# An AdaLN block on one core: the attention state two steps ahead, n1 + 1 for the column sums, new engine orders

## Chip, core and metric

One core of a Trainium2 chip runs the whole kernel. The metric is the device time of one execution in microseconds (us). The engines are TensorE (PE in the profile, its weight loads PEld), VectorE (DVE), ScalarE (ACT), GpSimd (POOL) and SyncE (SP), which issues most DMAs.

## What is computed

All data are float32: 16 sequences of 256 tokens, width 128.

```
mod = silu(c) @ wmod -> per sequence: sa, ca, ga, sb, cb, gb;  ga, gb kept at least 0.25 from 0
h  = LN(x) * (1 + ca) + sa
Q, K = elu(h@Wq + bq) + 1, elu(h@Wk + bk) + 1;  V = h@Wv + bv;  16 heads of 8
att = Q (K^T V) / (Q . sum_tokens K + 1e-6), per head
y  = LN(h + att@Wo + bo) * g1 + beta1
z  = LN(y + relu(y@W1 + b1)@W2 + b2) * g2 + beta2
x2 = x + ga * z
h2 = LN(x2) * (1 + cb) + sb;  mixes of h2 with the token before it, for receptance and key
out = x2 + gb * sigmoid(mix_r@Wr) * (relu(mix_k@Wk')^2 @ Wv')
```

## The kernel before

A sequence is two chunks of 128 tokens. `steps(step)` on each engine runs `step(t)` for t = 0 to 16, and each engine's `step` holds an order written out by hand; semaphores, counted by sequence, tie the engines together (`need`). Step t works on several sequences at once:

- sequence t, the front: n1 = LN(x) without its affine part (`next_n1`, scale from GpSimd's `norm_scale`), turned on TensorE (`transpose_in`, L932), `hT` by ScalarE (L284), keys (L1015 bias, L1018) and queries (L1023), `exp_k`, `exp_q`, `relu_q`, `k_sb`, `qT`. Then the state: n1^T k (L1049), the sum of k over tokens (GpSimd adds the two chunks into `k_pair`, L467, and TensorE multiplies by ones, L1060), ScalarE's `a_sb` (L328), the product with `wv_mod` (L1078), `kv_raw` by VectorE (L773: adds ksum times a row of `bv_row`), and GpSimd's two multiplies by the head mask into `kvs` (L475, L481).
- sequence t - 1, attention: reading the state (L1008), `den`, `rden`, `att`, turned, `attT` (L314), the projection with the residual (L937, L1055), statistics and `ny`.
- sequence t - 2, feed-forward: ny turned, `x1T` (L288), four hidden products (L975), `hid` by ScalarE (L311, L316, L320), the way out (L943), statistics of z.
- sequence t - 3: `centred`, `middle` (x2), n3.
- sequence t - 4, mix: n3 turned, three `keepT` of ScalarE (L273, L276), `mixT` of VectorE (L672), key (L962) and receptance (L966), relu, square, tanh, value (L1087), `prod`, `take_out`, store.

Of two neighbouring statistics and their aggregate VectorE mostly does something else between. Step 8 (MIX_AT) has two GpSimd operations, `mix_now` and `mix_prev`, for the end. Rows of bv and the gates come through DRAM: TensorE's small product, a store by SP, broadcast loads (`bv_row`, `gm_rows`) in BV_PARTS and GM_PARTS. The last sequences are drained by code of their own behind `steps`: sequence 13 by mixes, 14 and 15 by products with split weights on h2, and 15 in halves (`z_norm_of_last` and others). `keep_warm` multiplies a tile of ones to nothing.

## Time and profile before

| | us |
|---|---|
| median of 3 runs | 173.39 |
| lowest, highest | 173.34, 176.28 |
| the profiled execution | 173.09 |
| its span, first to last instruction | 171.4 |
| TensorE, VectorE, ScalarE, GpSimd busy | 160.8, 137.3, 107.3, 106.8 |

The span is counted from the first to the last instruction; some 1.7 us of the execution lie around it. A busy time sums an engine's instructions without their overlaps; a wait is given with what released it.

### The profile page before, as it was taken

To read this page: it belongs to the slowest core of one execution; us is meant where nothing else is said; L and a number is where in the kernel's file an instruction comes from. 1 tells how busy PE (TensorE), PEld (TensorE's weight loads), DVE (VectorE), ACT (ScalarE), POOL (GpSimd) and SP (SyncE) were. 2 spreads that over 40 slices of the span, in tenths; PEclk is the share of its full clock that TensorE was granted. 3 is DMA by queue.
4 is the path that set the end of the run, shared out by engine and by line. 5 is a ranking of instruction groups with operands and counts; after the bars stand their busy time and mean duration, and the time that the engine had idled before them with its cause. 6 is when DMAs were issued, how large, how long until landed. Compare 5 with 4: busy or idle time off the path is not lost. (4 is left out here: it accounts for less than half of the span.)

```text
span 171.4 us, 4095 instructions
## 1 busy us (share of the span) xinstructions
PE 160.8 (94%) x1181; PEld 148.7 (87%) x1181; DVE 137.3 (80%) x618; ACT 107.3 (63%) x294; POOL 106.8 (62%) x235
## 2 busy tenths in 40 slices
PE   7995899999999999999989999999999999998883
PEld 7784689889999999999979999999999999787672
DVE  3644885989797979889896979797989788777852
ACT  3152573839393949586774949493939495737552
POOL 5233435575677777767695868676777756683531
PEclk9999999999999999999999999999999999999999
DMA  4529929900010101000010101010101010010012
GB/s 134 193 57 345 306 69 299 399 11 4 2 34 0 31 0 33 4 12 22 0 33 0 33 4 33 0 34 0 33 0 34 0 32 4 2 31 25 6 34 61
DMA packets 8347, 10.08 MB, mean 59 GB/s; under 512 B 723, under 2 KB 6534, under 8 KB 8326
## 3 DMA queue, kind: packets, MB, share of 16 engines
q1 hardware_dynamic: 7856, 9.54, 17.6%
q10 hardware_dynamic: 438, 0.28, 0.6%
q8 instruction: 10, 0.16, 0.4%
q14 instruction: 11, 0.09, 0.2%
q0 software_dynamic: 32, 0.01, 0.0%
HBM read 7.69 MB, written 2.13 MB: 57 GB/s over the span
## 5 line engine op out<-in xcount | busy, mean ns | idle before, releaser
L943 PE MATMUL bank<-w,hid 128*128 128x128 f32 x240 | 31.4, 275 | 0.0
L284 ACT ACTIVATE hT<-bank,modT 128x256 f32<-128x256 f32 x16 | 9.0, 565 | 35.4 <-PE bank L932 35.4
L975 PE MATMUL bank<-x1T,w 128*128 128x256 f32 x120 | 30.9, 380 | 0.0
L943 PEld LDWEIGHTS bank<-w,hid 128*128 128x128 f32 x240 | 29.0, 192 | 0.0
L975 PEld LDWEIGHTS bank<-x1T,w 128*128 128x128 f32 x120 | 21.5, 190 | 2.5 <-ACT x1T L288 0.2
L432 POOL TENSOR_TENSOR rstd_n<-vare_n,power 128x2 f32<-128x2 f32 x30 | 21.3, 708 | 2.4
L430 POOL TENSOR_TENSOR vare_n<-mv_n,eps 128x2 f32<-128x2 f32 x30 | 6.0, 200 | 18.9 <-DVE mv_n L540 18.9
L546 DVE TENSOR_SCALAR ny<-bank,mv_ny,rstd_ny 128x128 f32<-128x128 f32 x32 | 11.7, 406 | 5.4 <-POOL rstd_ny L432 5.4
L276 ACT ACTIVATE keepT<-bank,modT 128x255 f32<-128x255 f32 x28 | 14.3, 563 | 0.6 <-PE bank L932 0.6
L531 DVE BATCH_NORM_STATS2 stats_z<-bank 128x6 f32<-128x128 f32 x30 | 7.4, 289 | 8.2 <-PE bank L943 8.1
L430 POOL TENSOR_TENSOR vare_z<-mv_z,eps 128x2 f32<-128x2 f32 x14 | 2.8, 197 | 17.9 <-DVE mv_z L540 17.9
L932 PE MATMUL bank<-ident,n 128*128 128x128 f32 x62 | 12.0, 275 | 1.0 <-DVE n L546 0.8
L320 ACT ACTIVATE hid<-bank,b_cols 128x256 f32<-128x256 f32 x30 | 12.7, 484 | 0.0
L450 POOL TENSOR_TENSOR out_sb<-x,prod 128x256 f32<-128x256 f32 x15 | 10.9, 728 | 2.1 <-DVE prod L667 2.0
L672 DVE SCALAR_TENSOR_TENSOR mixT<-bank,modT,keepT 128x256 f32<-128x256 f32 x28 | 12.1, 472 | 0.0
L1008 PE MATMUL bank<-kvs,qT 128*128 128x144 f32 x64 | 10.6, 288 | 1.5 <-issue 1.5
L432 POOL TENSOR_TENSOR rstd_ny<-vare_ny,power 128x2 f32<-128x2 f32 x16 | 11.1, 694 | 1.2
L1055 PE MATMUL bank<-kqvo,attT 128*128 128x128 f32 x64 | 11.5, 275 | 0.0
L647 DVE SCALAR_TENSOR_TENSOR x<-z,rstd_z,xb 128x128 f32<-128x128 f32 x30 | 10.8, 401 | 0.9 <-POOL out_sb L450 0.7
L300 ACT ACTIVATE exp_k<-bank,neg 128x256 f32<-128x256 f32 x16 | 7.7, 481 | 5.5 <-PE bank L1018 5.5
L443 POOL TENSOR_TENSOR xb<-x_all,gm_rows 128x256 f32<-128x256 f32 x15 | 10.9, 727 | 0.0
L1049 PEld LDWEIGHTS bank<-k_sb,n 128*128 128x128 f32 x64 | 9.5, 191 | 1.4 <-DVE k_sb L733 0.6
(176 smaller groups left out, 480.1 us busy)
## 6 DMA issues: line engine op xcount, KB each, us to landing
gm_rows<-mod_rows_dram SPq DMA_DIRECT2D x2, 960.0 KB, 9.0
out<-out_sb SPq DMA_DIRECT2D x15, 128.0 KB, 1.8
gm_rows<-mod_rows_dram SPq DMA_DIRECT2D x1, 768.0 KB, 6.2
w<-in_w SPq DMA_DIRECT2D x1, 512.0 KB, 4.9
bv_row<-bv_rows_dram SPq DMA_DIRECT2D x1, 512.0 KB, 11.7
x_all<-in_x SPq DMA_DIRECT2D x1, 384.0 KB, 4.4
bv_row<-bv_rows_dram SPq DMA_DIRECT2D x1, 384.0 KB, 5.5
gm_rows<-mod_rows_dram SPq DMA_DIRECT2D x1, 384.0 KB, 4.7
```

What stands on the lines that cost most here:

```text
L276: nc.scalar.activation(keepT[:, i, 1:L], banks[2][:, 0:L - 1], ACT.Identity, scale=mod_col(KEEP + i, s), bias=mod_col(SB, s)).then_inc((ke ...
L320: last = nc.scalar.activation(hid[:, f, :], hidden_bank(t)[:, (f - 2) * L:(f - 1) * L], ACT.Relu, bias=b1_cols[:, f:f + 1])
L432: nc.gpsimd.tensor_tensor(rstd[name][:, :], vare[name][:, :], power[:, :], ALU.pow).then_inc(rstd_ok[name], 1)
L443: nc.gpsimd.tensor_tensor(tile[:, :, :], x_all[:, NC * s:NC * (s + 1), :], gm_rows[:, s, GB_ROW:GB_ROW + 1, :].broadcast_to([128, NC, D]), ...
L450: nc.gpsimd.tensor_tensor(out_sb[s % 2][:, :, :], x2[s % 2][:, :, :], prod[:, :, :], ALU.add).then_inc(out_ok, 1)
L546: last = nc.vector.tensor_scalar(dest[:, c, :], source(c), mv[name][:, c, 0:1], rstd[name][:, c:c + 1], ALU.subtract, ALU.mult)
L647: last = nc.vector.scalar_tensor_tensor(x2[s % 2][:, c, :], z1[:, c, :], rstd["z"][:, c:c + 1], xb[:, c, :], ALU.mult, ALU.add)
L672: nc.vector.scalar_tensor_tensor(mixT[:, i, :], banks[2][:, 0:L], modT[:, MOVE + i, s:s + 1], keepT[:, i, :], ALU.mult, ALU.add).then_inc( ...
L932: last = nc.tensor.transpose(bank[:, c * 128:(c + 1) * 128], tile[:, c, :], ident[:, :])
L943: last = nc.tensor.matmul(banks[6][:, c * D:(c + 1) * D], hid[:, f, c * 128:(c + 1) * 128], w2[:, f, :], start=False, stop=(f == FF - 1 an ...
L975: return nc.tensor.matmul(bank[:, f % 2 * L:(f % 2 + 1) * L], w1[:, f * 128:(f + 1) * 128], x1T[:, :], start=True, stop=True)
L1055: last = nc.tensor.matmul(banks[1][:, c * D:(c + 1) * D], attT[:, c * 128:(c + 1) * 128], wo, start=False, stop=(c == NC - 1))
```

## The change

- **n1 + 1.** `first_scale` on GpSimd forms std and mean - std besides rstd, so that `take_n1` writes n1 + 1. Each token's row of n1 + 1 sums to 128, so the state product with a `wv_plus` of 144 columns (the last 16 are 1/128) yields ksum too. `k_pair`, the product with ones, `kv_raw` and both mask multiplies go; `plus_row` (GpSimd) adds bv's row to `wv_mod`, and `take_kvs` (VectorE) masks all 144 columns at once. The shift and bv's row are corrected by the same 1.
- **Two steps ahead.** The step works on t (front), t - 2 (attention), t - 3 (feed-forward), t - 4 (x2, n3), t - 5 (mix); `hT`, `qT`, `kvs`, `x2` have three buffers.
- **Orders.** All engines have new orders; step(t) runs for t = 4 to 17, and the first four steps are written out. Statistics and aggregate are one call (`y_norm`, `z_norm`, `n3_norm`, `first_stats`).
- **Start.** For sequences 0 and 1 wv_plus is formed directly (`direct_rows`, `direct_weights`); the products for the biases go ahead of the modulation; SP's loads have another order, and mix_w goes from ScalarE's queue to SP's. Several `keep_warm` go.
- **End.** Sequence 13 uses the split weights too; the order of the last pieces is new.

```diff
-BV_PARTS = ((0, 2), (2, 8), (8, 16))
+BV_PARTS = ((2, 4), (4, 9), (9, 16))
...
@@ sync
+            sp.dma_start(x_all[:, NC:2 * NC, :], x_dram[:, NC:2 * NC, :]).then_inc(x_in[1], 16)
             sp.dma_start(kqvo[:, 2:4, :], a["kqvo"][:, 2:4, :]).then_inc(wvo_loaded, 16)
-            sp.dma_start(x_all[:, NC:4 * NC, :], x_dram[:, NC:4 * NC, :]).then_inc(x_in[1], 16)
+            sp.dma_start(x_all[:, 2 * NC:4 * NC, :], x_dram[:, 2 * NC:4 * NC, :]).then_inc(x_in[2], 16)
             sp.dma_start(wmod[:, 2 * D:], a["wmod"][:, 2 * D:]).then_inc(wmod_loaded[1], 16)
+            sp.dma_start(w12[:, :, :], a["w12"]).then_inc(w12_loaded, 16)
+            sp.wait_ge(bv_ok, 1)
+            sp.dma_start(scratch["bv"], bv_rows[:, :]).then_inc(bv_stored, 16)
+            sp.dma_start(mix_w[:, :, :], a["mix_w"]).then_inc(mix_loaded, 16)
+            sp.wait_ge(bv_stored, 16)
+            load_bv(0)
+            sp.dma_start(x_all[:, 4 * NC:, :], x_dram[:, 4 * NC:, :]).then_inc(x_in[3], 16)
+            sp.wait_ge(rows_ok, 1)
+            sp.dma_start(scratch["rows"], mod_rows[:, :, :]).then_inc(rows_stored, 16)
+            load_bv(1)
+            sp.wait_ge(rows_stored, 16)
+            load_gm(0)
+            load_bv(2)
...
@@ scalar: head, then step
+            take_hT(0); exponent_k(0); take_hT(1)
+            act.wait_ge(bq_ok, 1)
+            exponent_q(0); take_a(0); positive_q(0); exponent_k(1)
...
+            take_x1T(0)
+            hidden(0, 0); hidden(0, 1); take_attT(1); hidden(0, 2); hidden(0, 3)
+            modulate_wv(4); modulate_wv(5)
+            step: take_x1T(sd) take_hT(sa) hidden(sd, 0) keeps(sc) take_attT(sb_) exponent_k(sa)
+                  hidden(sd, 1..3) positive_kk(sc) take_a(sa) square_kk(sc) exponent_q(sa)
+                  positive_q(sa) tanh_of_r(sc) modulate_wv(sa + 2)
...
@@ gpsimd
+            def first_scale(s):
+                nc.gpsimd.tensor_tensor(vare["n1"][:, :], mv["n1"][:, :, 1], eps[:, :], ALU.add).then_inc(vare_ok["n1"], 1)
+                nc.gpsimd.tensor_tensor(rstd["n1"][:, :], vare["n1"][:, :], power[:, :], ALU.pow).then_inc(rstd_ok["n1"], 1)
+                nc.gpsimd.tensor_tensor(std_n1[:, :], vare["n1"][:, :], rstd["n1"][:, :], ALU.mult).then_inc(std_ok, 1)
+                nc.gpsimd.tensor_tensor(mean_n1[:, :], mv["n1"][:, :, 0], std_n1[:, :], ALU.subtract).then_inc(mean_ok, 1)
+            def plus_row(s):
+                nc.gpsimd.tensor_tensor(wv_plus[s % 2][:, 0:D], wv_mod[s % 2][:, :], bv_row[:, s, :], ALU.add).then_inc(wvp_ok, 1)
-                    nc.gpsimd.tensor_tensor(k_pair[:, :], k_sb[:, 0, :], k_sb[:, 1, :], ALU.add).then_inc(pair_ok, 1)
+            step: norm_scale("z", sp_) take_out(sc - 1) gate_weights(sc) norm_scale("n3", sp_)
+                  plus_row(sa + 1) norm_scale("ny", sb_) x_plus_shift(sd) first_scale(sa + 2)
...
@@ vector: head in part, then step
+            def take_kvs(s):
+                need(dve, u_mm, s - 2)
+                need(dve, kv_mm, s + 1)
+                nc.vector.tensor_tensor(kvs[s % 3][:, :], banks[3][:, 0:D + H], mask[:, :], ALU.mult).then_inc(kvs_ok, 1)
+            take_n1(1); take_k(0); first_stats(2); take_q(0); direct_weights(1); take_kvs(0)
+            take_n1(2); take_k(1); denominators(0); attention(0); first_stats(3); take_q(1)
...
+            y_norm(1); shift_columns(); z_norm(0); take_ny(1)
+            step: centred(sp_) denominators(sb_) attention(sb_) middle(sp_) n3_norm(sp_) mixes(sc)
+                  take_k(sa) take_n3(sp_) y_norm(sb_) take_n1(sa + 1) first_stats(sa + 2)
+                  take_ny(sb_) take_kvs(sa) take_q(sa) z_norm(sd) gated(sc)
...
+            vare_of("z", whole, LAST); centred(s14); middle(s14); n3_norm(s14)
+            vare_of("n3", whole, LAST); z_norm_of_last(0); centred_last(0)
+            nc.vector.scalar_tensor_tensor(shift_n3[:, :], mv["n3"][:, :, 0], -1.0, rstd["n3"][:, :], ALU.mult,
+                                           ALU.mult).then_inc(shift_ok, 1)
+            z_norm_of_last(1); middle_last(0)
...
@@ tensor
+            def state(s):
+                need(pe, a_ok, s + 1)
+                nc.tensor.matmul(banks[3][:, 0:D + H], a_sb[:, :], wv_plus[s % 2][:, :], start=True, stop=True).then_inc(kv_mm, 1)
-                    nc.tensor.matmul(banks[3][:, D:D + 1], k_pair[:, :], ones[:, :], start=True, stop=True).then_inc(aks_mm, 1)
+            turn_n1(0); direct_rows(); bv_product(); key_of(0); query_of(0); turn_n1(1)
+            key_by_n1(0); key_of(1); state(0); query_of(1); turn_n1(2); read_state(0)
+            key_by_n1(1); second_modulation(); state(1); key_of(2); query_of(2); turn_att(0)
+            key_by_n1(2); projection(0); state(2); turn_n1(3); hidden_bias(); key_of(3)
+            query_of(3); turn_gates(); key_by_n1(3); state(3); turn_ny(0); read_state(1)
+            hidden_products(0); turn_att(1); feed_forward_out(0, 0, 2); projection(1)
+            feed_forward_out(0, 2, FF); turn_ny(1)
+            step: turn_n1(sa) read_state(sb_) hidden_products(sd) turn_att(sb_) key_of(sa)
+                  query_of(sa) projection(sb_) mix_key(sc) mix_receptance(sc) key_by_n1(sa)
+                  feed_forward_out(sd, 0, 2) state(sa) feed_forward_out(sd, 2, FF)
+                  value_product(sc) turn_ny(sb_) turn_n3(sp_)
...
+            key_of_h2(s13); turn_n3(s14); receptance_of_h2(s13); key_of_h2(s14)
+            value_product(s13); transpose_last(0); receptance_of_h2(s14); transpose_last(1)
+            key_last(0); value_product(s14); key_last(1); receptance_last(0)
+            value_last(0); receptance_last(1); value_last(1)
```

In the diff each call stands on a line of its own; several are written on one line here, and a step's order is given by its calls, with sa = t, sb_ = t - 2, sd = t - 3, sp_ = t - 4, sc = t - 5.

## Rows read from the trace of the kernel before

**Rows 1.** The page: busy time of each engine, and the granted clock in 40 slices

```profile
PE 160.8 (94%) x1181; PEld 148.7 (87%) x1181; DVE 137.3 (80%) x618; ACT 107.3 (63%) x294; POOL 106.8 (62%) x235
...
PEclk9999999999999999999999999999999999999999
```

**Rows 2.** Windows by stage: us, busy us (instructions) of each engine, PEclk, DMA, GB/s

```profile
6.80:46.10 39.30, 35.93 (x264) 32.01 (x264) 30.14 (x137) 21.73 (x56) 19.82 (x45) 1.00 0.50 164
46.10:145.80 99.70, 98.86 (x760) 94.68 (x760) 86.95 (x390) 70.38 (x198) 71.26 (x157) 1.00 0.06 16
```

**Rows 3.** Timeline of TensorE, steady steps: start us, us, engine, line, op, tiles, count

```profile
46.15 0.38 PE L932 MATMUL bank<-ident,n 128*128 128x128 f32 x2
...
55.12 0.38 PE L932 MATMUL bank<-ident,n 128*128 128x128 f32 x2
...
97.31 0.28 PE L1060 MATMUL bank<-ones,k_pair 128*128 128x1 f32 x2
97.45 0.68 PE L962 MATMUL bank<-mixT,mix_w 128*128 128x256 f32 x2
97.96 0.61 PE L966 MATMUL bank<-mix_w,mixT 128*128 128x128 f32 x4
...
98.62 0.39 PE L1078 MATMUL bank<-wv_mod,a_sb 128*128 128x128 f32 x2
98.85 1.06 PE L943 MATMUL bank<-w,hid 128*128 128x128 f32 x8
...
103.22 1.46 PE L975 MATMUL bank<-x1T,w 128*128 128x256 f32 x6
104.51 0.38 PE L932 MATMUL bank<-ident,att 128*128 128x128 f32 x2
```

**Rows 4.** Timeline of all engines, a steady step and the drain

```profile
73.27 0.49 DVE L531 BATCH_NORM_STATS2 stats_z<-bank 128x6 f32<-128x128 f32 x2 [0.67 <-PE bank L943]
...
73.68 0.40 DVE L667 SCALAR_TENSOR_TENSOR prod<-tanh_r,bank 128x256 f32<-128x256 f32 x1
...
74.01 0.56 ACT L288 ACTIVATE x1T<-bank,beta_b,cols 128x256 f32<-128x256 f32 x1
...
75.45 0.48 ACT L300 ACTIVATE exp_k<-bank,neg 128x256 f32<-128x256 f32 x1
...
146.97 1.56 PE L975 MATMUL bank<-x1T,w 128*128 128x256 f32 x6
...
154.68 0.48 DVE L531 BATCH_NORM_STATS2 stats_z<-bank 128x6 f32<-128x128 f32 x2
...
155.27 0.25 DVE L540 BATCH_NORM_AGGREGATE mv_z<-stats_z 128x2 f32<-128x6 f32 x2
```

**Rows 5.** Groups of GpSimd instructions by line and shape, us, mean ns, idle before

```profile
L432 POOL TENSOR_TENSOR rstd_n<-vare_n,power 128x2 f32<-128x2 f32 x30 | 21.3, 708 | 2.4
...
L481 POOL TENSOR_TENSOR kvs<-kv_raw,headmask 128x128 f32<-128x128 f32 x16 | 7.3, 456 | 3.1 <-DVE kv_raw L773 2.9
...
L430 POOL TENSOR_TENSOR vare_ny<-mv_ny,eps 128x2 f32<-128x2 f32 x16 | 3.3, 204 | 2.6 <-DVE mv_ny L540 2.6
```

**Rows 6.** Timeline of TensorE, step 8: the column sum

```profile
88.23 0.38 PE L1060 MATMUL bank<-ones,k_pair 128*128 128x1 f32 x2 [0.84 <-POOL k_pair L467]
```

**Rows 7.** Timeline of all engines, start

```profile
7.35 0.56 ACT L284 ACTIVATE hT<-bank,modT 128x256 f32<-128x256 f32 x1 [4.05 <-PE bank L932]
...
10.04 0.71 PE L1049 MATMUL bank<-k_sb,n 128*128 128x128 f32 x4 [0.36 <-DVE k_sb L733]
...
13.92 0.35 DVE L773 SCALAR_TENSOR_TENSOR kv_raw<-bv_row,a_sb,bank 128x128 f32<-128x128 f32 x1 [2.54 <-DMA bv_row<-bv_rows_dram]
...
14.90 0.73 PE L1008 MATMUL bank<-kvs,qT 128*128 128x144 f32 x4 [1.46 <-issue]
```

**Rows 8.** Timeline of all engines, end

```profile
158.88 0.29 DVE L788 BATCH_NORM_STATS2 stats_z<-bank 128x6 f32<-128x128 f32 x1
...
168.99 0.29 DVE L839 TENSOR_TENSOR out_last<-x_end,prod_last 128x128 f32<-128x128 f32 x1
```

More of the change, by code:

```diff
@@ L49, in build @@
         mix_w = sb("mix_w", [128, 3, D])
-        wrT, wkT, wvT = (mix_w[:, i, :] for i in range(3))
+        wvT = mix_w[:, 2, :]
         cols = sb("cols", [128, COLS])
@@ L210, in build @@
         block = ctx.enter_context(nc.Block())
+        s13, s14 = LAST - 2, LAST - 1
+        whole, half = slice(0, NC), [slice(c, c + 1) for c in range(NC)]
         @block.sync
@@ new lines, in hidden, with keeps @@
+            def hidden(s, f):
+                if f % 2 == 0:
+                    need(act, (w1a_mm, w1b_mm)[f // 2], s + 1)
+                bank = (banks[7], banks[6])[f // 2]
+                ins = nc.scalar.activation(hid[:, f, :], bank[:, f % 2 * L:(f % 2 + 1) * L], ACT.Relu, bias=b1_cols[:, f:f + 1])
+                if f % 2 == 1:
+                    ins.then_inc((hida_ok, hidb_ok)[f // 2], 1)
+            def keeps(s):
+                need(act, mix_ok, s)
+                need(act, h2T_mm, s + 1)
+                nc.scalar.activation(keepT[:, :, 0:1], modT[:, FIRST:FIRST + 2, s:s + 1], ACT.Copy)
+                for i in range(2):
+                    last = nc.scalar.activation(keepT[:, i, 1:L], banks[2][:, 0:L - 1], ACT.Identity, scale=mod_col(KEEP + i, s),
+                                                bias=mod_col(SB, s))
+                last.then_inc(keep_ok, 1)
@@ new lines, in turn_att, with projection @@
+            def turn_att(s):
+                need(pe, att_ok, s + 1)
+                need(pe, hT_ok, s + 3)
+                need(pe, reluk_ok, s - 3)
+                transpose_in(banks[0], att, attT_mm)
+            def projection(s):
+                need(pe, attT_ok, s + 1)
+                for c in range(NC):
+                    residual_into(banks[1], hT[s % 3], c)
+                    last = nc.tensor.matmul(banks[1][:, tokens(c)], attT[:, tokens(c)], wo, start=False, stop=(c == NC - 1))
+                last.then_inc(y_mm, 1)
@@ L941, in feed_forward_out, with hidden_products @@
+            def hidden_products(s):
+                for f in range(FF):
+                    hidden_product(s, f, (banks[7], banks[6])[f // 2])
+            def feed_forward_out(s, f0, f1):
+                if f0 == 0:
+                    need(pe, hidb_ok, s + 1)
+                    for c in range(NC):
+                        residual_into(banks[6], x1T, c)
                 for f in range(f0, f1):
                     for c in range(NC):
-                        last = nc.tensor.matmul(banks[6][:, c * D:(c + 1) * D], hid[:, f, c * 128:(c + 1) * 128], w2[:, f, :],
-                                                start=False, stop=(f == FF - 1 and c == NC - 1))
```

1332 lines of the change are left out of this document (708 added, 624 removed).

## The prediction

> **What bounds the kernel now.** I began with the page [rows 1]: TensorE is busy 94% of the span, VectorE 80%, ScalarE and GpSimd some 62%; the clock stays at the upper level, 2.4 GHz. I then cut the span into stages [rows 2]. From 46.1 to 145.8 us TensorE is busy 98.86 of 99.70 us; from 6.8 to 46.1 it is busy 35.93 of 39.30 us, and part of that are products that only keep it busy. Two neighbouring rows of the turning of n1 stand 8.97 us apart [rows 3]: that is the steady period. So there only work taken off TensorE, or an engine that becomes slower than it, moves the time; at both ends it is the waits.
>
> **Steady step.** The column-sum product and its successor need 0.14 us (97.31 to 97.45) and 0.51 us (97.45 to 97.96) [rows 3]. Two passes of 256 columns alone take a third of 1.30 us, 0.43 us, as six pass in that time (the attention rows follow 1.29 us behind the hidden ones). So the sum costs 0.14 + 0.08 = 0.22 us, of which I take 0.21. The state product's two passes of 128 columns take 0.23 us (98.62 to 98.85); with 144 it is an eighth more, 0.03 us. The new period is 8.97 - 0.21 + 0.03 = 8.79 us, if nothing waits.
>
> Does anything wait? Counted from the new step's first instruction, TensorE reads the state at 0.22, starts the hidden products at 0.71, turns attention at 2.44, projects at 3.64, mixes at 4.31, multiplies key by n1 at 5.18, the state at 6.73, and turns ny at 8.31. A result must be there some 0.15 us ahead: after a wait the load is exposed (six passes take 1.56 instead of 1.46 us) and the release costs 0.05 [rows 4].
> - x1T: turning ny ends at 8.69; ScalarE's 0.56 us and the release give 9.34. Due 9.34. No slack.
> - attT: ScalarE takes hidden 0 at 1.78, then three keeps (1.44 us from x1T's start at 74.01 to exp_k's at 75.45, of which I give x1T 0.45: 0.99 us [rows 4]), then attT until 3.52; due 3.49. Loss 0 to 0.05 us.
> - k_sb: VectorE mixes from 3.27, takes k and ends at 4.5; the receptance product of the mix needs its bank at 4.7. Slack 0.15 to 0.2.
> The state itself is now two steps ahead and has whole microseconds.
>
> VectorE works 86.95 us in this stage of 11.12 steps, 7.8 us a step [rows 2]. The multiply that replaces kv_raw has about its size. But statistics and their aggregate now stand side by side in all four norms, and so do den, reciprocal and attention. An instruction that depends on nothing starts 0.41 us behind a pair of statistics (73.27 to 73.68); a dependent one 0.59 us (154.68 to 155.27) [rows 4]; with one wait in place of two I take 0.54. Four times 0.13 is 0.5 us: 8.3 of 8.79 us. It still fits, with waits of 0.5 us in all; below, a rival starts here. The bounds: 0 and 4 x 0.18 + 0.2 = 0.9 us.
>
> The Trainium skill ("VectorE: DVE Perf Modes", section on the DRAIN you can't avoid) says that the pipe empties behind every operation and that a semaphore adds nothing to it. By that rule the new order would cost VectorE nothing. The trace differs (0.41 against 0.59 us), so the measurement decides.
>
> GpSimd loses the mask multiply of kvs (456 ns), the pair sum of the same size and the small one for the sums, and gains std and mean at about the 200 ns of vare each, and wv_plus at 456 ns [rows 5]: 0.1 to 0.3 us less. In step 8 its two mix_now operations hold the column sum and TensorE for 0.84 us and a further 0.3 us of lateness [rows 6]; no sum hangs behind them now, but z's rstd does. I keep 0.5 of 1.1 us. ScalarE has the same work in another order.
>
> **Start.** TensorE now waits for wq and bq's product first, then the modulation; n1 of step 0 needs std and mean too. I put hT(0) at 8.0 against 7.35 us [rows 7]. The bv round trip, for which VectorE and TensorE wait 2.54 and 1.46 us [rows 7], is gone: direct rows serve steps 0 and 1. SP's reordered loads (x of step 1 ahead of Wv and Wo, w12 early, mix_w behind the bv store) all land ahead of their new users; if one does not, only the later x blocks, whose 1.5 MB stand behind a store, could cost 1 us. But the order by hand opens other waits. GpSimd's four dependent operations, 0.27 + 0.75 + 0.26 + 0.20, give a mean 1.5 us behind the aggregate (durations of 0.20 and 0.71 [rows 5] and a release of 0.05 each). VectorE stands at take_n1(1) until 10.6 and only then takes k(0), ready at 9.9: it gets out at 11.5 (before, TensorE used it at 10.04 [rows 7]). Carried through the queues with the durations above, TensorE waits:
> n1(1) 1.6; hT(1) 0.3; n1(2) 1.2; a(1) 0.3; k(2) 0.6; k(3) 0.5; a(3) 0.8; x1T(0) 0.4; the second half of hidden(0), which ScalarE takes behind attT(1), 1.5; ny(1), whose statistics, scale and normalising form one chain behind projection(1) and behind shift_columns and z_norm(0) in VectorE's queue, 2.4; step 4 0.6. Sum 10.2 us.
> Against that stands useful work only. By its passes (0.22 us for two of 128 columns, 0.43 for two of 256, as above) a front is 1.89, an attention 1.60, a feed-forward 3.73 and a mix 1.53 us; five fronts, three attentions and two feed-forwards are 21.7 us, the modulation, bias, gate and direct products 4.4. From 7.5 this gives 7.5 + 21.7 + 4.4 + 10.2 = 43.8 us for the start of step 5. The kernel before starts its step 5 at 46.15 [rows 3], but by then has done one attention, one feed-forward and one mix more: 6.8 us. So the start loses 6.8 - 2.35 = 4.5 us.
>
> **Sum.** Steps 5 to 15 are eleven: 43.8 + 11 x 8.79 + 0.5 = 141.0 us for the start of step 16.
>
> **End.** There remain two attentions, three feed-forwards, five mixes and doubled products for three sequences instead of two, 24.4 us of TensorE work against 17.2. Now ScalarE does keeps between hidden(0) and attT with no front to fill it: twice 1.0 us. x1T follows turn_ny at once: 0.2, 0.2 and 0.7. The last feed-forward waits for ScalarE 0.3. I reach the statistics of the last z's first half 20.1 us behind that start, at 161.1; before they stood at 158.88 [rows 8]. From there the chain to the last add took 10.4 us before [rows 8]. Now shift_n3 stands behind z_norm_of_last(0), so n3(14), its turning and h2 come after; but the key and receptance of 13 fill TensorE meanwhile, and value(14) waits for a square that ScalarE does behind both halves of h2(15). I reach 10.7. End at 141.0 + 30.8 = 171.8 us, against 169.3. The same store follows.
>
> The profiled execution took 173.09 us (span 171.4), 0.3 us under the median of 173.39, less than the runs differ among themselves; I make no correction: 173.09 + 2.5 = **175.6 us**. In parts: start +4.5, steady -11 x 0.18 - 0.6 = -2.6, end +0.6. My own bounds for the first are +2 to +6, for the last -1 to +2.5. A measurement of this kernel can tell about 2% (3.5 us) from no change: under 169.9, over 176.9.
>
> **Rivals.**
> 1. VectorE becomes the bound. If the side-by-side dependencies cost 0.9 us and the waits for u and keeps don't shift together, a step is 9.1 us: 11 x 0.31 = 3.4 more, 179.0 us. For it: 8.3 of 8.79 us full, and attT, x1T with no slack. Against: nothing forces the waits to add. It decides from a period above 8.97. Chance 0.20.
> 2. The start is as dense as before, and the whole is faster. If the chain at n1(1) and the one at ny(1) are shorter than I have them, and TensorE's holes in the start are no larger than today's, the 4.5 us fall away: 171.1 us. It decides where the start loses under 2.0 us. For it: the bv stall is gone and the state is early. Against: eleven named waits. Below 169.9 it comes only with a shorter end as well. Chance 0.24.
> 3. The cut isn't worth what the rows say: the period stays 8.97, as passes elsewhere stretch or attT's 0.05 and x1T's wait come in each step: +2.0, 177.6 us. Chance 0.08.
> 4. The holes bring TensorE's clock down. Before, the hole of 1.46 us left it at 2.4 GHz [rows 1, 7], with extra products put in between; the new start has fewer of them and holes of 1.5 and 2.4 us. At 1.2 GHz passes take twice as long, so one step's worth (8.8 us) done at half rate for 3 us costs 1.5 to 3: 178.0 us. No row shows the lower level. Chance 0.04.
> The Trainium skill ("TensorE: Matmul & The Clock Gate", section on what's actually happening) holds that an idle array falls to half rate and that activity lifts it again. The trace of before, never below full, can't show the fall.
>
> **How the numbers follow.** My forecast has 0.44, with its own range 173.5 to 177.5. The range of 8 in 10 reaches down to rival 2's 171.0 and up to 178.8. Faster by over 2%: half of rival 2's spread below and little else, 0.11. Slower: rival 1 (0.18), rivals 3 and 4 (0.07), the top of the forecast (0.03): 0.28. Within 2%: 0.61.
>
> **What would show it.** A period of turning n1 of 8.79 us with TensorE full shows the cut right; 9.0 or more with VectorE idle near zero shows rival 1. hT(1) at 11.8, exp_k(3) at 23 and step 5's turn at 43.8 test the start; idle rows of TensorE behind hid and ny rows of about 1.5 and 2.4 us test the two largest holes. In the end, attT waits of 1 us in steps 16 and 17, statistics of the last z at 161. The forecast is wrong if the start's holes sum to under 7 or over 13 us, or if a steady row waits in every step.

## The result, and the profile after

The change made the kernel slower: 183.16 us median (181.24 to 184.5, 4 runs) against 173.45 for the kernel before in the same series. The ratio is 1.048 (95% interval 1.0435 to 1.052); every ratio here is formed from the runs within 1.5% of the fastest of their kernel, which for the changed kernel are only 181.24 and 182.08. I had forecast 175.6 us, range 171.0 to 178.8. The profiled execution took 184.5 us, the longest of the four; its span is 182.8. What follows explains that execution; where the two shorter ones gained their 3 us was not recorded.

Page of the kernel after, busy time of each engine and the granted clock in 40 slices:

```profile
PE 167.7 (92%) x1147; PEld 147.5 (81%) x1147; DVE 146.1 (80%) x623; ACT 106.9 (58%) x290; POOL 103.6 (57%) x233
...
PEclk9999999969999999999999999999999999999999
```

Against [rows 1], TensorE has 34 instructions fewer and is busy 6.9 us longer, and VectorE is busy 8.8 us longer. One slice of the clock, some 37 to 41 us into the span, is no longer 9. The windows of the kernel after, to the start of step 5, from there to the start of step 16, the end, and one steady step (us, busy us and instructions of TensorE, its weight load, VectorE, ScalarE, GpSimd; clock, DMA share, GB/s):

```profile
0.00:47.10 47.10, 39.21 (x225) 32.86 (x226) 29.21 (x145) 18.74 (x48) 17.55 (x51) 0.96 0.52 164
47.10:148.70 101.60, 100.32 (x739) 90.69 (x737) 93.71 (x387) 70.89 (x196) 69.12 (x152) 1.00 0.05 14
148.70:182.80 34.10, 28.15 (x188) 23.95 (x186) 23.22 (x93) 17.29 (x47) 16.93 (x31) 1.00 0.08 24
111.97:121.04 9.07, 9.07 (x69) 8.26 (x68) 8.68 (x37) 6.45 (x18) 6.47 (x15) 1.00 0.05 14
```

All three parts came later than forecast: step 5 at 47.05 us instead of 43.8, step 16 at 148.7 instead of 141.0, and the last add ends 31.7 us behind that instead of 30.8. The three errors are 3.25, 4.45 and 0.9 us, which is 8.6 of the 8.9 us between the forecast and the profiled execution.

**The steady period.** It is the distance between rows of turning, which answer to [rows 3] (the four passes of a row here turn n3 and then n1; the rows begin steps 7 to 10, and a step proper begins 0.22 us later, with n1):

```profile
64.90 0.60 PE L1058 MATMUL bank<-ident,n 128*128 128x128 f32 x4
73.99 0.60 PE L1058 MATMUL bank<-ident,n 128*128 128x128 f32 x4
83.26 0.60 PE L1058 MATMUL bank<-ident,n 128*128 128x128 f32 x4
93.83 0.60 PE L1058 MATMUL bank<-ident,n 128*128 128x128 f32 x4
```

Over the whole stage the distance is mostly 9.01 to 9.09 us, where I had 8.79 and the kernel before 8.97; it is 9.27 and 9.37 once each, and 10.57 from step 9 to step 10, behind GpSimd's work at the end of its step 8. VectorE's timeline in one step of 9.07 us shows no wait at all in its rows:

```profile
111.78 0.49 DVE L629 BATCH_NORM_STATS2 stats_z<-bank 128x6 f32<-128x128 f32 x2
112.30 0.25 DVE L636 BATCH_NORM_AGGREGATE mv_z<-stats_z 128x2 f32<-128x6 f32 x2
...
113.50 0.35 DVE L689 RECIPROCAL rden<-den 128x32 f32<-128x32 f32 x1
113.96 0.49 DVE L695 TENSOR_TENSOR att<-bank,rden 128x128 f32<-128x128 f32 x2
114.36 0.81 DVE L728 SCALAR_TENSOR_TENSOR x<-z,rstd_z,xb 128x128 f32<-128x128 f32 x2
...
117.14 0.65 DVE L642 TENSOR_SCALAR n<-x,mv_n,rstd_n 128x128 f32<-128x128 f32 x2
117.72 0.48 DVE L629 BATCH_NORM_STATS2 stats_ny<-bank 128x6 f32<-128x128 f32 x2
118.23 0.25 DVE L636 BATCH_NORM_AGGREGATE mv_ny<-stats_ny 128x2 f32<-128x6 f32 x2
118.40 0.57 DVE L663 TENSOR_SCALAR n<-x_all,mean_n,rstd_n 128x128 f32<-128x128 f32 x2
118.89 0.48 DVE L629 BATCH_NORM_STATS2 stats_n<-x_all 128x6 f32<-128x128 f32 x2
...
119.65 0.73 DVE L642 TENSOR_SCALAR ny<-bank,mv_ny,rstd_ny 128x128 f32<-128x128 f32 x2
```

Note what the window says of the same step: TensorE busy 9.07 of 9.07 us, VectorE 8.68. Read alone, that says TensorE bounds the step. It does not: with the same products the steady step takes 8.77 us in another kernel below. A short wait ahead of a weight load does not show in the busy time, since the ends of TensorE's products are modelled.

**The start.** TensorE's timeline, the waits over 1 us that I had named, and what follows the longest:

```profile
16.96 0.44 PE L1058 MATMUL bank<-ident,n 128*128 128x128 f32 x2 [1.01 <-DVE n L663]
...
31.98 0.44 PE L1063 MATMUL bank<-ident,x1T 128*128 128x128 f32 x2 [1.26 <-ACT hid L321]
...
36.90 0.44 PE L1058 MATMUL bank<-ident,ny 128*128 128x128 f32 x2 [2.04 <-DVE ny L642]
...
38.05 3.52 PE L1142 MATMUL bank<-x1T,w 128*128 128x256 f32 x8
...
47.76 1.94 PE L1142 MATMUL bank<-x1T,w 128*128 128x256 f32 x8
```

The holes are there, near their forecast sizes of 1.2, 1.5 and 2.4 us. But the hidden products behind the third take 3.52 us, and 1.94 in the next step. The granted clock is 0.50 from 38 to 41 us. Eight passes at half rate, 1.2 GHz, are rival 4, which I had given 0.04. The very first products run at half rate too:

```profile
5.59 0.58 PE L1197 MATMUL bank<-cols,kqvo 128*128 128x1 f32 x2 [0.69 <-DMA kqvo<-in_kqvo]
...
8.93 0.66 PE L1058 MATMUL bank<-ident,n 128*128 128x128 f32 x2 [0.23 <-DVE n L844]
...
10.91 1.22 PE L1078 MATMUL bank<-kqvo,hT 128*128 128x128 f32 x4
...
14.28 0.71 PE L1078 MATMUL bank<-kqvo,hT 128*128 128x128 f32 x4
```

In the kernel before hT(0) was taken at 7.35 [rows 7], behind n1(0) turned at 6.87; here n1(0) is turned at 8.93, and four passes take 1.22 us until about 13 us, then 0.71. The clock's column reads 1.00 for this first stretch, so the half rate is read from the durations. The kernel before begins at half rate as well: two warming products take 0.77 us at 5.41 and 0.49 at 6.54, so there the rate rose at about 6 us. "Never below full", as the prediction has it, is what the column said and not what the rows say.

### The profile page after: what moved, and what is told of

It reads as the page before. It is cut to its first block, busy times and chain, and to the rows that moved or that the text cites. A ratio compares the mean times of both kernels' runs of the same rounds, so it can differ in the third digit from the quotient of the medians.

```text
span 182.8 us, 4107 instructions
## 1 busy us (share of the span) xinstructions
PE 167.7 (92%) x1147; PEld 147.5 (81%) x1147; DVE 146.1 (80%) x623; ACT 106.9 (58%) x290; POOL 103.6 (57%) x233
## 4 chain that ended last, share of the span: by engine, by line
PE 55%; DVE 26%; issue 6%; ACT 5%; POOL 4%; DMA 2%; SPq 0%; DVEq 0%; POOLq 0%; ACTq 0%
PE bank L1142 11%; PE bank L1158 9%; PE bank L1058 5%; PE bank L1180 3%; PE bank L1078 3%; PE bank L1063 3%; PE bank L1190 3%; PE bank L1114 3%; DVE stats_n L629 2%; PE bank L1173 2%; PE bank L1128 2%; PE bank L1097 2%; DVE x L728 2%; DMA kqvo<-in_kqvo 2%; DVE mixT L745 2%
## 5 line engine op out<-in xcount | busy, mean ns | idle before, releaser
L1142 PE MATMUL bank<-x1T,w 128*128 128x256 f32 x128 | 32.9, 402 | 0.7 <-ACT x1T L314 0.7
L321 ACT ACTIVATE hid<-bank,b_cols 128x256 f32<-128x256 f32 x60 | 25.2, 479 | 13.8 <-PE bank L1142 13.8
L1142 PEld LDWEIGHTS bank<-x1T,w 128*128 128x128 f32 x128 | 24.0, 198 | 4.8 <-ACT x1T L314 1.8
L314 ACT ACTIVATE x1T<-bank,beta_b,cols 128x256 f32<-128x256 f32 x16 | 9.0, 565 | 23.4 <-PE bank L1058 23.4
L504 POOL TENSOR_TENSOR vare_ny<-mv_ny,eps 128x2 f32<-128x2 f32 x16 | 3.4, 210 | 27.0 <-DVE mv_ny L636 27.0
L512 POOL TENSOR_TENSOR rstd_n<-vare_n,power 128x2 f32<-128x2 f32 x15 | 13.6, 907 | 1.2
L728 DVE SCALAR_TENSOR_TENSOR x<-z,rstd_z,xb 128x128 f32<-128x128 f32 x30 | 12.2, 446 | 1.6 <-POOL rstd_z L506 1.1
L504 POOL TENSOR_TENSOR vare_n<-mv_n,eps 128x2 f32<-128x2 f32 x14 | 2.8, 197 | 16.4 <-DVE mv_n L636 16.4
L1058 PE MATMUL bank<-ident,n 128*128 128x128 f32 x62 | 10.7, 284 | 1.5 <-DVE n L663 1.0
L1128 PE MATMUL bank<-kqvo,attT 128*128 128x128 f32 x64 | 11.5, 275 | 0.0
L1097 PE MATMUL bank<-k_sb,n 128*128 128x128 f32 x64 | 10.3, 285 | 0.8 <-DVE k_sb L670 0.8
L1114 PE MATMUL bank<-kvs,qT 128*128 128x144 f32 x64 | 10.6, 289 | 0.0
L1078 PE MATMUL bank<-kqvo,hT 128*128 128x128 f32 x64 | 10.6, 290 | 0.0
```

The costliest lines, as they stand in the source:

```text
L321: ins = nc.scalar.activation(hid[:, f, :], bank[:, f % 2 * L:(f % 2 + 1) * L], ACT.Relu, bias=b1_cols[:, f:f + 1])
L512: nc.gpsimd.tensor_tensor(rstd["n1"][:, :], vare["n1"][:, :], power[:, :], ALU.pow).then_inc(rstd_ok["n1"], 1)
L728: last = nc.vector.scalar_tensor_tensor(x2[s % 3][:, c, :], z1[:, c, :], rstd["z"][:, c:c + 1], xb[:, c, :], ALU.mult, ALU.add)
L1058: last = nc.tensor.transpose(bank[:, tokens(c)], tile[:, c, :], ident[:, :])
L1078: nc.tensor.matmul(banks[4][:, tokens(c)], hT[s % 3][:, tokens(c)], wk, start=(c == 0), stop=False)
L1097: last = nc.tensor.matmul(banks[3][:, 0:D], n1[s % 2][:, c, :], k_sb[:, c, :], start=(c == 0), stop=(c == NC - 1))
```

## The experiments

Each ratio is to the kernel before, in runs on the same chip. The changed kernel run again is the base of the first group.

**0. The changed kernel again** (no edit).

> The changed kernel again, unchanged, for a profile beside its variants. All theories: 181 to 184.5 us, steady period 9.07 us (turning of n1), a hole of about 2 us ahead of turning ny(1) and, behind it, the lower TensorE clock for about 3.5 us; the raise of the clock near the start as late as 13 us instead of 6. If the runs' difference of 3 us is the clock's alone, the lowered stretch lies elsewhere or is longer or shorter in this profile.

Measured: 183.81 us, ratio 1.057 (1.050 to 1.064). Periods mostly of 9.0 to 9.1, step 5 at 47.6. The steady step repeats; the clock does not. This time the first products were at the full rate at 5.85 us, and the granted clock was at 0.50 three times: from 8 to 11.5 us, from 18.3 to 21.7 (2.4 us behind a wait of 1.01 for n1(2)) and from 38.8 to 42.2, behind the hole at ny(1).

**1. Filling TensorE's holes in the start.**

```diff
-            keep_warm(WARM)
+            keep_warm(WARM + 4)
...
             feed_forward_out(0, 2, FF)
+            keep_warm(9)
             turn_ny(1)
```

> Four more products of ones in the wait for wq at the start, nine in the hole ahead of turning ny(1); nothing else. Theory clock: TensorE is at 2.4 GHz from about 7 us on and never falls; 1.8 us come back behind ny(1) and 2 to 2.5 at the start, together 3 to 4.5 us less than the changed kernel. Rival (the start is set by the chains through VectorE and GpSimd, the clock only fills their shadow): under 1 us less. Both: steady period unchanged, 9.07.

Measured: 182.00 us, 1.049 (1.043 to 1.055), 1.8 us less than the changed kernel, though the two intervals overlap. TensorE's timeline (the program's nine products are 18 of the profile's):

```profile
34.76 2.17 PE L1018 MATMUL bank<-warm 128*128 128x128 f32 x18
36.96 0.44 PE L1058 MATMUL bank<-ident,ny 128*128 128x128 f32 x2
...
38.11 1.99 PE L1142 MATMUL bank<-x1T,w 128*128 128x256 f32 x8
```

With products in the hole the eight passes behind it take 1.99 us instead of 3.52. The Trainium skill ("TensorE: Matmul & The Clock Gate", section on what's actually happening) says that an idle array drops to half rate; these rows agree. It does not drop every time. The hole of 2.04 us stands unfilled in nine profiles of this document; in seven the eight passes behind it take 2.89 to 3.52 us, in those of experiments 2 and 10 they take 1.99. What decides it is not shown.

The expectation held in this one place only. At the start the first products now run at the full rate from 5.64 us, but the clock fell to 0.50 from 18 to 21.6 us instead, and the wait at n1(1) grew from nothing to 1.39: n1(4) is turned at 37.23, no earlier than the 37.17 before. So the 3 to 4.5 us of the expectation were not there.

**2. VectorE's old order, statistics and aggregates apart.** An independent instruction stands between the statistics and the aggregate of n3, y, x and z again; of these the place of y's:

```diff
-                    y_norm(sb_)
+                    need(dve, y_mm, sb_ + 1)
+                    norm_stats("ny", lambda c: y[:, c, :])
+                if live(sa + 2):
...
+                    norm_stats("n1", x_chunk(sa + 2))
+                if live(sb_):
+                    norm_mv("ny", sb_ + 1)
```

> In VectorE's step alone, statistics and aggregate are taken apart again (the half of the mix, the statistics of the next x and the gated product stand between). Theory VectorE-bound by dependent neighbours: VectorE is 0.4 us freer, the receptance product of the mix no longer waits, and the period falls from 9.07 to 8.80 +- 0.05; the whole is 2.5 to 3.5 us less. Rival (VectorE is late because ScalarE's keeps come late, or because its operations stretch beside GpSimd): period 9.0 or more, under 1 us less.

Measured: 190.93 us, 1.096 (1.087 to 1.105). That is 7 us slower. VectorE now waits twice in every step:

```profile
100.04 0.65 DVE L642 TENSOR_SCALAR n<-x,mv_n,rstd_n 128x128 f32<-128x128 f32 x2 [0.47 <-POOL rstd_n L506]
...
102.80 0.73 DVE L642 TENSOR_SCALAR ny<-bank,mv_ny,rstd_ny 128x128 f32<-128x128 f32 x2 [0.53 <-POOL rstd_ny L506]
```

An aggregate taken later gives GpSimd the variance later, and VectorE stands at the scaling. So GpSimd's answer is a term of VectorE's step. The cost of the dependent neighbours is not refuted by this: from one n3 pair to the next it is 9.71 us, and without the two waits of 0.47 and 0.53 it is 8.71, or 0.36 less than 9.07. That is the 0.4 us expected; the waits took back more than twice as much. The two waits are where the theory of experiments 6 and 7 comes from.

**3. The mixing weights multiplied out in the head instead of step 8.**

```diff
-                if t == MIX_AT:
-                    nc.gpsimd.tensor_tensor(mix_now[:, :, :], mix_w[:, 0:2, :],
...
+            pool.wait_ge(mix_loaded, 16)
+            nc.gpsimd.tensor_tensor(mix_now[:, :, :], mix_w[:, 0:2, :],
...
             norm_scale("ny", 2)
```

> mix_now and mix_prev (GpSimd) go from the end of step 8 to the start, where GpSimd waits anyway. Theory (step 8's extra 1.5 us of period, 10.57 for 9.07, is GpSimd's delay handed on through z's scale): 1.3 to 1.5 us less and no longer step. Rival (it is absorbed because later steps catch up): under 0.4 us less.

Measured: 182.27 us, 1.048 (1.0405 to 1.055), 1.5 us less, which the intervals alone would not show, but the rows do. The step that took 10.57 us takes 9.07 (84.86 to 93.93). In the kernel after the two operations stand ahead of z's scale, and VectorE waits for it:

```profile
84.20 0.61 POOL L586 TENSOR_TENSOR mix_now<-mix_w,cols 128x256 f32<-128x256 f32 x1
84.89 0.73 POOL L590 TENSOR_TENSOR mix_prev<-mix_w,mix_now 128x256 f32<-128x256 f32 x1
...
86.78 1.17 DVE L728 SCALAR_TENSOR_TENSOR x<-z,rstd_z,xb 128x128 f32<-128x128 f32 x2 [1.05 <-POOL rstd_z L506]
```

**4. The same move alone in the kernel before** (step 2 instead of 8).

```diff
-MIX_AT = 8
+MIX_AT = 2
...
                 if t == MIX_AT:
+                    pool.wait_ge(mix_loaded, 16)
```

> The kernel before with the mixing weights multiplied out at step 2 instead of step 8, nothing else. If the 0.84 us stall of TensorE behind k_pair in step 8 is all that the block costs in the kernel before, this takes about 1.1 us off it: 172.3. If the block fills a gap that another wait would fill anyway, or delays something of the start as much, 173.4, no change.

Measured: 172.26 us, 0.993 (0.9905 to 0.996): 1.1 us less, as [rows 6] said.

**5. The arithmetic of the change alone, in the kernel before.** The engine orders, the one-step pipeline and the order of the start are those of before. What belongs to the arithmetic comes along: the direct rows for sequences 0 and 1, which spare the start the round trip of bv through DRAM, and `wv_mod` a step earlier on ScalarE. The three places of the steady step:

```diff
-                    need(pe, pair_ok, sa + 1)
-                    nc.tensor.matmul(banks[3][:, D:D + 1], k_pair[:, :], ones[:, :], start=True, stop=True).then_inc(a_mm, 1)
...
-                    nc.tensor.matmul(banks[3][:, 0:D], a_sb[:, 0:D], wv_mod[:, :], start=True, stop=True).then_inc(kv_mm, 1)
+                    nc.tensor.matmul(banks[3][:, 0:D + H], a_sb[:, :], wv_plus[sa % 2][:, :], start=True, stop=True).then_inc(kv_mm, 1)
...
-                    nc.vector.scalar_tensor_tensor(kv_raw[:, :], bv_row[:, sa, :], ksum, banks[3][:, 0:D],
-                                                   ALU.mult, ALU.add).then_inc(kvs_ok, 1)
+                    nc.vector.tensor_tensor(kvs[:, :], banks[3][:, 0:D + H], mask[:, :], ALU.mult).then_inc(kvs_ok, 1)
```

> The arithmetic part of the change alone, put into the kernel before: n1 plus one, the sums over keys read from 16 constant columns of wv_plus, no k_pair, no product for the column sums, no kv_raw; the engine orders, the pipeline depth and the start stay as before. Theory (the arithmetic is sound, the new orders and the start lose the time): TensorE bounds the period here, it loses the column-sum product and gains 16 columns, so 8.97 goes to 8.8 and the whole to about 171 (0.985). Rival (what slows VectorE lies in the arithmetic, for instance in GpSimd's longer scale): the period stays at 8.97 or rises and the whole is 173.4 or more.

Measured: 170.18 us, 0.973 (0.967 to 0.980). The four executions took 168.34 to 173.51, and the ratio rests on the lower two, 168.34 and 169.08. This half of the change is faster, by 2 to 3%. In the profile it is 4.3 us: step 5 begins at 44.87 instead of 46.15, ten ordinary steps are 0.2 us shorter each, the step behind GpSimd's mixing weights 0.7 us (9.37 for 10.08), and the rest lies behind step 16. Its window of one steady step:

```profile
98.09:106.86 8.77, 8.77 (x69) 8.41 (x68) 7.84 (x36) 6.39 (x18) 6.15 (x14) 1.00 0.06 17
```

The period is 8.77 us, my 8.79. The product count is the same 69 as in the 9.07 us step of the kernel after, and VectorE is busy 7.84 us, 0.84 less. Some of its rows in that step:

```profile
98.29 0.50 DVE L544 BATCH_NORM_STATS2 stats_z<-bank 128x6 f32<-128x128 f32 x2 [0.48 <-PE bank L983]
98.70 0.40 DVE L701 SCALAR_TENSOR_TENSOR prod<-tanh_r,bank 128x256 f32<-128x256 f32 x1
...
99.93 0.32 DVE L751 RECIPROCAL rden<-den 128x32 f32<-128x32 f32 x1
100.17 0.51 DVE L671 SCALAR_TENSOR_TENSOR z<-bank,mv_z,gm_rows 128x128 f32<-128x128 f32 x2
```

Something independent starts 0.41 us behind the statistics and 0.24 behind the reciprocal; in the kernel after the dependent instruction starts 0.52 and 0.46 behind them.

**6. Two ways to relieve VectorE.** First, ten waits of VectorE dropped whose order other waits give; three of them:

```diff
             def take_k(s):
-                need(dve, a_mm, s)
                 need(dve, expk_ok, s + 1)
...
             def middle(s):
-                need(dve, xb_ok, s + 1)
-                need(dve, out_ok, s - 2)
                 need(dve, z1_ok, s + 1)
```

> The changed kernel with ten waits of VectorE dropped whose order other waits already give (of take_k, take_q, take_kvs, attention, take_ny, take_n3, mixes, take_n1 one each, of the middle pair two). Theory A (a second wait ahead of a VectorE instruction costs some 0.08 us even when it is long fulfilled): the steady period falls from 9.07 to about 8.8 to 8.5 by that many waits and then meets TensorE, the whole from 183.8 to about 180. Theory B (a fulfilled wait is free, VectorE's instructions themselves are longer than I summed): period 9.07, 183.8.

Measured: 181.74 us, 1.049 (1.041 to 1.057); periods of 9.00 (111.41, 120.41, 129.42). In an ordinary step ten waits are worth at most 0.07 us together, against the 0.08 us for each that theory A had: it fell. The two longer steps, 9.27 and 9.37, are 9.00 here too, so that steps 5 to 15 took 1.0 to 1.3 us less than in the two profiles of the changed kernel.

Second, the scaling of x to n1 moved to ScalarE:

```diff
+            def scale_n1(s):
+                need(act, a_mm, s - 1)
+                need(act, mean_ok, s)
+                for c in range(NC):
+                    last = nc.scalar.activation(n1[s % 2][:, c, :], x_all[:, NC * s + c, :], ACT.Identity,
+                                                scale=rstd["n1"][:, c:c + 1], bias=mean_n1[:, c:c + 1])
...
-                if live(sa + 1):
-                    take_n1(sa + 1)
                 if live(sa + 2):
+                    need(dve, mean_ok, sa + 1)
                     first_stats(sa + 2)
```

> The changed kernel with the pair that scales x to n1 moved from VectorE (0.49 us of its queue in a step) to ScalarE, from sequence 5 on; GpSimd's two small products become one product and one subtraction from one, and the order of the rest stays. Theory (VectorE bounds the steady period): it falls by 0.3 us, to where TensorE takes over at 8.75 to 8.8, and the whole from 183.8 to about 180. Rival (the bound is a loop of waits through GpSimd's scales, and VectorE only looks full): the period stays at 9.0 to 9.07.

Measured: 183.15 us, 1.055 (1.047 to 1.063); periods mostly of 9.06. VectorE lost 0.49 us of work per step and the step did not move. VectorE's timeline says why:

```profile
109.32 0.25 DVE L653 BATCH_NORM_AGGREGATE mv_ny<-stats_ny 128x2 f32<-128x6 f32 x2
109.48 0.45 DVE L646 BATCH_NORM_STATS2 stats_n<-x_all 128x6 f32<-128x128 f32 x2
...
110.73 0.73 DVE L659 TENSOR_SCALAR ny<-bank,mv_ny,rstd_ny 128x128 f32<-128x128 f32 x2 [0.51 <-POOL rstd_ny L517]
```

From mv_ny to ny it is 1.41 us, and in the kernel after 1.42 (118.23 to 119.65). The stretch is GpSimd's round trip. In the kernel after n1 and the next statistics fill it to 0.1 us, so VectorE looks full; n1 taken out leaves a wait of its size.

**7. The last kernel again, with the statistics of y ahead of the n3 pair.**

```diff
-                if live(sp_):
-                    take_n3(sp_)
                 if live(sb_):
                     y_norm(sb_)
+                if live(sp_):
+                    take_n3(sp_)
```

> n1 scaled by ScalarE as in the run before (period 9.07 there, VectorE 0.51 us idle ahead of ny, waiting for GpSimd's rstd_ny), and VectorE's statistics of y put ahead of the n3 pair, nothing else. Theory (the period is VectorE's queue outside the stretch mv_ny to ny, plus that stretch, which is never shorter than GpSimd's round trip of about 1.25 us): the n3 pair now lies inside the stretch, the idle 0.51 goes, and the period falls to where TensorE bounds it, 8.75 to 8.8; the whole from 183.2 to about 180. Rival (something else holds the period at 9.07, such as TensorE's hidden products or contention between VectorE and GpSimd): the idle time turns up elsewhere and the period stays at 9.0 or more.

Measured: 180.03 us, 1.038 (1.036 to 1.041); periods mostly of 8.82 to 8.83 (109.40, 118.23). VectorE's rows:

```profile
114.72 0.25 DVE L653 BATCH_NORM_AGGREGATE mv_ny<-stats_ny 128x2 f32<-128x6 f32 x2
114.88 0.57 DVE L659 TENSOR_SCALAR n<-x,mv_n,rstd_n 128x128 f32<-128x128 f32 x2
115.37 0.48 DVE L646 BATCH_NORM_STATS2 stats_n<-x_all 128x6 f32<-128x128 f32 x2
...
116.14 0.73 DVE L659 TENSOR_SCALAR ny<-bank,mv_ny,rstd_ny 128x128 f32<-128x128 f32 x2
```

Again 1.42 us from mv_ny to ny, now filled by the n3 pair, and no wait. One pair to another engine did nothing, and one pair into the gap it left gave 0.24 us a step. That settles the steady part: in the kernel after the period is VectorE's queue outside this stretch plus the stretch itself, which GpSimd's round trip does not let shrink below 1.42 us. With the queue shortened TensorE bounds again, 0.03 above my 8.79: VectorE's only wait in a step, of 0.18 us, is for TensorE's product, and of the chain that ended last 73% is TensorE's, against 55 and 42% in the two profiles of the changed kernel. The new order without n1 on ScalarE was not run.

**8. The start's first products in the old order.**

```diff
+            pe.wait_ge(silu_ok, 2)
+            pe.wait_ge(wmod_loaded[0], 16)
+            modulation_columns(banks[1], (1, 0))
+            keep_warm(1)
             pe.wait_ge(kq_loaded, 16)
             pe.wait_ge(cols_loaded, 16)
             nc.tensor.matmul(banks[6][:, 0:1], wq, cols[:, BO:BO + 1], start=True, stop=True)
...
-            pe.wait_ge(silu_ok, 2)
-            pe.wait_ge(wmod_loaded[0], 16)
-            modulation_columns(banks[1], (1, 0))
-            keep_warm(2)
+            keep_warm(1)
```

(and VectorE's bias steps behind n1(0), to match).

> The changed kernel with the first products in the order of the kernel before: TensorE's modulation columns ahead of the two bias products, VectorE's modT and n1(0) ahead of the bias steps. Theory (the late start, n1(0) turned at 8.9 instead of 7.5, and TensorE at its lower clock until 13 us, come from the 0.69 us hole behind the warming passes while kqvo lands, and from the modulation columns behind it): n1(0) is turned at about 7.5, the passes are at the full clock there, and step 5 begins 1.4 to 2.5 us earlier; the whole from 183.8 to about 182. Rival (the later loads and GpSimd's scale of n1(1) set the start): hT(1) stays at 13.7 and step 5 at 47; 183.8.

Measured: 182.59 us, 1.054 (1.051 to 1.057), 1.2 us less than the changed kernel, with intervals that overlap. In the profile n1(0) is turned at 6.56 instead of 8.93, with the full clock, and step 5 begins at 44.9. But a new hole opens:

```profile
10.97 0.44 PE L1058 MATMUL bank<-ident,n 128*128 128x128 f32 x2 [2.02 <-DVE n L663]
...
12.06 1.22 PE L1078 MATMUL bank<-kqvo,hT 128*128 128x128 f32 x4
```

and the clock falls behind it (0.50 from 12 to 15 us). Step 5 comes 2.1 us earlier than in the kernel after, by the profiles; the medians moved less.

**9. Everything mended at once.** Experiments 7, 8, 3 and the nine products of 1.

> The changed kernel with all that was found: n1 scaled by ScalarE and statistics of y ahead of n3, the start's first products in the old order, nine warming passes ahead of turning ny(1), mixing weights multiplied out in the head. By the sum of the parts: 183.8 minus 3.2 (period 8.78, 11 steps) minus 1.8 (clock behind ny(1)) minus 1.5 (step 8) minus 1.5 (start) = about 176; that is still over the kernel before, since the start as a whole and the deeper pipeline's end stay. If the two-step pipeline itself costs nothing, 173 or less.

Measured: 176.12 us, 1.016 (1.015 to 1.018), near the sum of the parts. The changed design, mended, is still 1.6% behind the kernel before. A further mend of the start, the statistics of x(1) ahead of the bias steps and four products ahead of turning n1(1):

> The kernel with all parts mended (176.1), and in its start VectorE's statistics of x(1) ahead of the bias steps and four warming passes ahead of turning n1(1), where TensorE stood for 1.99 us and its clock was lower from 11.5 to 15. Theory (waits and the clock of the first 43 us are what is left of the start's loss): n1(1) is turned at about 10 instead of 11.05, the granted clock keeps its upper level, step 5 begins about 2 us earlier, the whole is about 174. Rival (the later sequences' loads and scales set the start, so a gain at n1(1) is lost by sequence 2 or 3): 176.

Measured: 176.05 us, 1.009 (1.004 to 1.013); the chip of this call ran the kernel before at 174.23. In the profile the clock is at its upper level throughout, n1(1) is turned at 10.67, and step 5 begins at 42.7. I had expected n1(1) at 10 and 2 us at step 5; it was 0.4 earlier at n1(1) and 0.8 at step 5 than in the run before (43.5), and the medians are the same. The time is the rival's 176, not the theory's 174.

**10. GpSimd's sum moved away from VectorE's x pair** (in the changed kernel).

```diff
-                if live(sc - 1):
-                    take_out(sc - 1)
...
+                if live(sc - 1):
+                    take_out(sc - 1)
                 if live(sb_):
                     norm_scale("ny", sb_ + 1)
```

> The changed kernel with GpSimd's 128x256 sum out_sb (0.73 us) moved from beside VectorE's x pair to ahead of GpSimd's scale of ny; VectorE's queue is untouched. Theory (the two engines slow each other while both read SBUF: the x pair takes 0.82 us in two instructions there, 0.61 in the kernel before): the x pair goes back to about 0.61 to 0.65 and the period falls by about 0.2 to 8.87, the whole by 2 us to 181.5. Rival (the x pair is slower for another reason, or the sum lies in GpSimd's round trip for ny, which then lengthens): period 9.07 or more.

Measured: 184.83 us, 1.059 (1.051 to 1.068); periods of 9.27. Half of the expectation holds. Here are VectorE's x and n3 pairs and GpSimd's sum:

```profile
104.37 0.60 DVE L728 SCALAR_TENSOR_TENSOR x<-z,rstd_z,xb 128x128 f32<-128x128 f32 x2
...
106.93 1.07 DVE L642 TENSOR_SCALAR n<-x,mv_n,rstd_n 128x128 f32<-128x128 f32 x2
```

```profile
107.19 0.73 POOL L539 TENSOR_TENSOR out_sb<-x,prod 128x256 f32<-128x256 f32 x1
```

The x pair fell from 0.81 to 0.60 and the n3 pair beside the moved sum rose from 0.65 to 1.07. The net is +0.21 us, and the period rose by 0.20. The slowing was beside GpSimd's sum in both places, so contention between the two engines is shown, at 0.2 to 0.4 us a step. And both pairs lie outside the stretch from mv_ny to ny: there VectorE's work moves the period one for one. I had only asked which instruction it would leave.

**11. The best version: experiments 4 and 5 together.**

> The kernel before with the arithmetic of the change (as in the run that gave 170.2) and the mixing weights multiplied out at step 2 (alone 172.3). If both gains add, 170.2 minus 1.1 = 169.1, ratio 0.967 to the kernel before.

Measured: 168.80 us (168.14 to 170.4), 0.975 (0.970 to 0.980): the lowest median of all, in the old orders with the new arithmetic. The 1.1 us expected on top of experiment 5 are not shown: the ratios are 0.975 and 0.973, and the median of 170.18 there has two long executions in it. In the rows the step of 9.37 us is gone (8.77), which is 0.6 us.

## Why the prediction was wrong

**The cut: right.** "The new period is 8.79, if nothing waits." Experiment 5 has 8.77.

**VectorE's part of the steady step: the step that failed.** I wrote 7.8 + 0.5 = 8.3 of 8.79 us, "it still fits". Measured: VectorE is busy 8.68 us, 0.86 more than 7.8 and at the upper bound of 0.9 that I had kept, and 0.39 us of gaps too short to be listed as waits stand between its instructions; together that is the period of 9.07. Counted from the start of each instruction to the start of the next, VectorE's queue without its waits is 7.91 us in experiment 5 and 9.06 in the kernel after. The 1.15 us between them are:
- statistics and aggregate side by side, four times: 0.34. This is my 0.5, and it was too high.
- den, reciprocal and attention side by side: 0.32. I had named them, and the sum has nothing for them.
- the x pair beside GpSimd's out_sb, 0.85 for 0.64: 0.21 (experiment 10). I had taken durations from rows in which VectorE worked beside other work of GpSimd.
- the n3 pair and the gap ahead of it, at a scale that GpSimd ends at 117.03, 0.1 us ahead of the pair: 0.23.
- the rest: 0.05.

And I counted as if only the sum mattered, while the queue runs through GpSimd's 1.42 us (experiments 6 and 7). This is rival 1 nearly as written, 9.1 us "with VectorE idle near zero", at a chance of 0.20; the dependent neighbours, which it gives as the cause, are 0.34 to 0.66 us of the 1.15. At 9.07 and with the steps of 9.27 and 9.37 us the period is 3.5 us of the 4.45.

**GpSimd's block in step 8.** "I keep 0.5 of 1.1 us": the block cost 1.5 (experiment 3), the other 1.0 of the 4.45. The wait moved from TensorE's column sum to z's rstd, which I had named and priced at a third.

**The start.** I wrote 7.5 + 21.7 + 4.4 + 10.2 = 43.8. The windows of TensorE from turning n1(0) to step 5, the kernel after first, then the start mended:

```profile
8.93:47.05 38.12, 32.27 (x197) 26.92 (x197) 25.76 (x118) 17.03 (x44) 14.88 (x38) 0.96 0.49 158
```

```profile
6.84:42.70 35.86, 31.66 (x224) 27.18 (x224) 25.90 (x119) 17.65 (x46) 16.23 (x43) 1.00 0.56 184
```

- n1(0) was turned at 8.93 instead of 7.5: +1.4. "hT(0) at 8.0" left out that the first product, wq's for the biases (L1197), waits 0.69 us for its weights and that the passes behind it run at half rate.
- The holes sum to 38.12 - 32.27 = 5.9 us instead of 10.2: -4.3. The two largest were right to 0.4 us. The 1.6 us at n1(1) did not appear, since passes at half rate filled them (at the full rate 1.39 us stood there, experiment 1), and each of the others was smaller than I had it. "Under 7" was my own sign that the forecast is wrong.
- The useful passes take 28.4 us at the full clock (31.66 less 3.2 of filling products in the mended run) instead of 26.1: +2.3. An exposed load behind a wait, which I had used for the steady step and not here, is some 0.05 us each (eight passes 1.99 for 1.94), so it is a small part of this; the rest is open.
- The clock: 32.3 - 28.4 = +3.9, where rival 4 had 1.5 to 3. I had it at 0.04 because the hole of 1.46 us in [rows 7] did not bring it down; in that kernel filling products stood just ahead of the hole, and the new start has none there. Whether they are the reason was not tested. Some 1.5 us of the 3.9 are the eight passes behind ny(1); the passes before 13 us partly filled holes, as experiment 1 shows, and their net price was not separated.

The four sum to +3.3, which gives the 47.05 measured. That the start loses was right and rival 2 fell; that the sum missed by only 3.3 is in part luck, since holes forecast 4.3 us too large hid more than half of what the late n1(0), the passes and the clock added (7.6).

**The end.** Right to 0.9 us: statistics of the last z's first half stand at 169.76, 21.1 us behind step 16, forecast 20.1; and from there to the end of the last add it is 10.6, forecast 10.7:

```profile
169.76 0.30 DVE L930 BATCH_NORM_STATS2 stats_z<-bank 128x6 f32<-128x128 f32 x1 [0.17 <-PE bank L1336]
...
180.10 0.29 DVE L982 TENSOR_TENSOR out_last<-x,prod_last 128x128 f32<-128x128 f32 x1
```

What stays behind in experiment 9 can be placed against experiment 11, whose profile is 8.1 us shorter (spans 174.2 and 166.1). The deeper pipeline turns n1(5) with one attention, one feed-forward and one mix less behind it, 6.86 us of passes at the prediction's prices. It does so only 1.1 us earlier (43.5 and 44.6), so the start loses 5.7 us; the ten steps to n1(15) lose 1.2; and from there to the end 41.9 us remain instead of 33.8, 8.1 more, of which 6.86 are that same work, so the end loses 1.2. By this estimate most of the loss lies in the start and not in the drain. The depth without the hand-written start was not tried, so whether the depth itself costs anything stays open.

## What to carry to other kernels

To ask whether an engine fits into a step, sum its queue from start to start of its instructions, not its busy time: here that was 9.06 us against 8.68. Then take some work off it; if a wait of the same size appears, the work lay in a loop through another engine, whose answer must be filled with work or asked for earlier. Test each half of a change alone before making both: the arithmetic here, with its direct rows, was worth 2.7% and lay hidden under orders and a start that cost more than twice that. A duration read beside one neighbour is not a price beside another, and work moved in time takes its contention with it.
